# One transposing load for two pairs of expert tiles instead of one

## The reference, cut to what matters

```python
def layer0(x, t_emb, router_W, router_bias, w1, w3, w2, W1e, W2e):
    xf = x.reshape(-1, 256)                                   # 8192 tokens
    shared = silu(xf @ w1) * (xf @ w3) @ w2                   # every token
    s = sigmoid(concat([xf, tf], -1) @ router_W)              # 8 experts
    _, topk_idx = top_k(s + router_bias, 2)                   # two experts a token
    combine = ...                                             # gates of the two, which sum to 1
    y = einsum('enh,ehc->enc', gelu(einsum('nc,ech->enh', xf, W1e)), W2e)
    routed = einsum('ne,enc->nc', combine, y)
    return (shared + routed) / 3

def layer1(h, z, W, b, alpha):                                # z is the layer before's output
    def step(h, z_t):                                         # 256 steps, one after the other
        gate = sigmoid(h @ Wh.T + z_t @ Wz.T + b)
        h = tanh(h * (1 - alpha) + gate * z_t)
        return h, h

x = x + layer0(x, cond, ...)
x = x + layer1(cond, x, ...)
```

## Time and profile before

| | |
|---|---|
| time, median of 3 runs | 770.74 us (768.95 to 771.95) |
| the profiled execution | 774.02 us, of which the span of instructions is 772.1 us |
| mean granted clock of TensorE | 0.967 |
| PE busy | 711.0 us (92%) |
| DVE, ACT, POOL busy | 549.0, 472.3 and 270.6 us |
| DMA moved | 124.83 MB, 162 GB/s over the span |
| transposing loads of `xe` | 88 |

### The profile page before, as it was taken

One profiled execution on the slowest core, in us unless ns is written; L12 is line 12 of the kernel. 1 busy time (PEld: TensorE's weight loads), 2 busy tenths in 40 slices (PEclk: granted clock), 3 DMA queues, 4 the chain that ended last, 5 costly groups with the idle time before them and its releaser, 6 DMA issues.

```text
span 772.1 us, 23818 instructions
## 1 busy us (share of the span) xinstructions
PE 711.0 (92%) x8562; PEld 512.1 (66%) x8562; DVE 549.0 (71%) x2014; ACT 472.3 (61%) x1347; POOL 270.6 (35%) x284
## 2 busy tenths in 40 slices
PE   5899898998999999999989999999999999999763
PEld 3454486645788756898568896565888555686442
DVE  4787651458777698876678886897975678866754
ACT  4746464634567755677666677556876645676433
POOL 2037455166542156452075025772040173003100
PEclk9999999999999999999999999999999999999865
DMA  8836799774996675895859454357484354123101
GB/s 279 323 110 226 222 235 281 199 193 117 205 233 167 172 174 141 203 213 164 205 144 253 99 146 165 118 166 132 101 203 135 111 164 118 43 90 121 39 14 42
DMA packets 166466, 124.83 MB, mean 162 GB/s; under 512 B 118706, under 2 KB 147156, under 8 KB 166356
## 3 DMA queue, kind: packets, MB, share of 16 engines
q1 hardware_dynamic: 150436, 79.19, 42.1%
q0 software_dynamic: 14368, 41.96, 17.7%
q10 hardware_dynamic: 1552, 2.15, 0.8%
HBM read 39.90 MB, written 55.84 MB: 124 GB/s over the span
## 4 chain that ended last, share of the span: by engine, by line
PE 68%; DVE 12%; ACT 7%; DMA 6%; issue 4%; SPq 1%; POOL 1%; ACTq 0%; DVEq 0%; POOLq 0%
PE bank L1731 64%; PE bank L1930 2%; DMA xe<-x_slots_even 2%; PE bank L1865 1%; DVE full L1492 1%; DVE pre L1553 1%; DVE hid_low L1499 1%; DVE taken L1550 1%; SPq L956 1%; DMA xe<-x_slots_odd 1%; ACT th L1249 1%; ACT hs_high L1257 1%; DMA x_res<-in_x_dram 1%; POOL y_got L1129 1%; DVE r_sum L1518 1%
## 5 line engine op out<-in xcount | busy, mean ns | idle before, releaser
L1731 PE MATMUL bank<-xe,w1e_high 128*128 128x128 f16 x1360 | 216.6, 220 | 8.1 <-DMA xe<-x_slots_even 3.6
L1731 PE MATMUL bank<-xs,w_high 128*128 128x512 f16 x512 | 168.9, 385 | 5.0 <-DVE w_low L1669 2.8
L1731 PE MATMUL bank<-xe,w1e_low 128*128 128x128 f16 x680 | 146.9, 219 | 0.0
L1499 DVE TENSOR_TENSOR hid_low<-full,hid_high 128x512 f16<-128x512 f32 (+1 forms) x152 | 103.2, 679 | 45.1 <-ACT hid_high L1202 34.9
L1731 PEld LDWEIGHTS bank<-xe,w1e_high 128*128 x1360 | 114.3, 97 | 26.5 <-issue 14.0
L1249 ACT ACTIVATE th<-bank 128x64 f32<-128x64 f32 x256 | 56.9, 222 | 101.4 <-PE bank L1731 97.3
L1550 DVE SCALAR_TENSOR_TENSOR taken<-th,zq 128x64 f32<-128x64 f32 x256 | 58.2, 227 | 78.0 <-ACT th L1249 73.6
L1257 ACT ACTIVATE hs_high<-pre 128x64 f16<-128x64 f32 x256 | 65.5, 256 | 73.7 <-DVE pre L1553 62.5
L1731 PEld LDWEIGHTS bank<-hs_high,gwt_high 128*128 128x128 f16 x1024 | 70.1, 97 | 51.9 <-ACT hs_high L1257 37.5
L1070 POOL TENSOR_TENSOR fence_pool<-zero 128x1 f32<-128x1 f32 x12 | 2.8, 234 | 278.2 <-DMA y_slots_odd<-y_pair 84.7
L1731 PE MATMUL bank<-hs_high,gwt_high 128*128 128x32 f16 x1024 | 79.0, 178 | 22.5 <-ACT hs_high L1257 21.9
(11 more groups left out here) (156 smaller groups left out, 1705.8 us busy)
## 6 DMA issues: line engine op xcount, KB each, us to landing
y_slots_even<-y_pair SPq DMA_DIRECT2D x45, 256.0 KB
y_slots_odd<-y_pair SPq DMA_DIRECT2D x37, 256.0 KB
x_res<-in_x_dram SPq DMA_DIRECT2D x16, 512.0 KB
out_dram<-o_tok SPq DMA_DIRECT2D x32, 256.0 KB, 3.1
x_tok<-in_x_dram SPq DMA_DIRECT2D x14, 512.0 KB, 5.0
x_slots_even<-zeros POOLq DMA_DIRECT2D x1, 4096.0 KB, 18.1
x_slots_odd<-zeros POOLq DMA_DIRECT2D x1, 4096.0 KB, 15.2
y_got<-in_L_cond_W1e_dram SPq DMA_DIRECT2D x4, 512.0 KB, 12.9
```

What stands on the lines that cost most here:

```text
L1499: dve.tensor_tensor(hid[1][:, u.i % NR, some], full32[:, u.i % 2, some], hid[0][:, u.i % NR, some], ALU.subtract).then_inc(s_lo, 1)
L1731: return pe.matmul(out_ap, w, mov, start=start, stop=stop, skip_group_check=True)
```

## The change

One load now brings two pairs, 512 rows (the last one of a section 384, as the last pair has one tile). The ring of four pairs becomes two halves of two pairs, with one semaphore a half. Loads are issued at odd pairs only, once the second pair of the half has been read, so that the loads of pairs k + 3 and k + 4 are issued together in the unit with the odd pair k. `first_pairs` issues two loads in place of four. PE waits for the half's load ahead of each of its pairs.

```diff
-        xe = sb("xe", [P, NIN, 2, KC, 2 * P], F16)
+        xe = sb("xe", [P, NIN // 2, 2, KC, 4 * P], F16)
...
-        s_xin = [sem(f"s_xin{i}") for i in range(NIN)]
+        s_xin = [sem(f"s_xin{i}") for i in range(NIN // 2)]
...
-            def load_pair(n, p):
+            def load_pairs(n, p):
                 nth = PAIR0[n] + p
                 if nth >= NIN:
-                    sp.wait_ge(s_up, PAIR_UNIT[nth - NIN] + 1)
-                rows = P if p == PAIRS[n] - 1 else 2 * P
-                sp.dma_start_transpose(xe[:, nth % NIN].rearrange("p h k s -> p (h k) s")[:, :, 0:rows],
-                                       x_slots[n % 2][2 * p * P:2 * p * P + rows, :]).then_inc(s_xin[nth % NIN], 16)
+                    sp.wait_ge(s_up, PAIR_UNIT[nth - NIN + 1] + 1)
+                rows = 3 * P if p == PAIRS[n] - 2 else 4 * P
+                sp.dma_start_transpose(xe[:, nth // 2 % 2].rearrange("p h k s -> p (h k) s")[:, :, 0:rows],
+                                       x_slots[n % 2][2 * p * P:2 * p * P + rows, :]).then_inc(s_xin[nth // 2 % 2], 16)
             def first_pairs(n):
                 scattered(sp, n)
-                for p in range(NIN):
-                    load_pair(n, p)
+                for p in range(0, NIN, 2):
+                    load_pairs(n, p)
...
-                if u.kind == EXPERT and u.k + NIN < PAIRS[u.n]:
-                    load_pair(u.n, u.k + NIN)
-                elif u.kind == EXPERT and u.n + 1 < NS and follows(u.n + 1):
-                    if u.k + NIN == PAIRS[u.n]:
-                        scattered(sp, u.n + 1)
-                    load_pair(u.n + 1, u.k + NIN - PAIRS[u.n])
+                if u.kind == EXPERT and u.k % 2 == 1:
+                    if u.k - 1 + NIN < PAIRS[u.n]:
+                        load_pairs(u.n, u.k - 1 + NIN)
+                    elif u.n + 1 < NS and follows(u.n + 1):
+                        if u.k - 1 + NIN == PAIRS[u.n]:
+                            scattered(sp, u.n + 1)
+                        load_pairs(u.n + 1, u.k - 1 + NIN - PAIRS[u.n])
...
-                    pe.wait_ge(s_xin[up.nth % NIN], (up.nth // NIN + 1) * 16)
+                    pe.wait_ge(s_xin[up.nth // 2 % 2], (up.nth // NIN + 1) * 16)
```

More of the change, by code:

```diff
@@ L1762, in up_part @@
                 return mm(up_bank(u)[:, (h * tiles_of(u) + i) * P:(h * tiles_of(u) + i + 1) * P], w1e_s[a][k][h][:, experts[u.k % 4, i], :],
-                          xe[:, u.nth % NIN, c, k, i * P:(i + 1) * P], k == 0 and n == 0, k == 1 and n == 2)
+                          xe[:, u.nth // 2 % 2, c, k, (u.nth % 2 * 2 + i) * P:(u.nth % 2 * 2 + i + 1) * P],
+                          k == 0 and n == 0, k == 1 and n == 2)
             def down_part(u, i, h, n):
```

## The result

The changed kernel takes 789.88 us (median of 4 runs, 787.96 to 791.45) against 770.92 us before (4 runs): a ratio of 1.025, 95% interval 1.021 to 1.029. The time lies in the stated range, 3.9 us above the 786 that were forecast. The profiled execution took 790.9 us with a span of 789.0 us, 16.9 us more than the span before. The ratios further down leave out three slow executions: one of doubles_from_1_load_first (1691.87 us) and two of the kernel before (776.28 and 777.17 us).

A forecast was written before the change was run, and what follows sets the result against it. PE, busy 92% of the span, was taken to bound the kernel. Waits of 16.2 us plus 1.6 for the clock less 2.5 gave 15.3 us, on the median 770.7 a forecast of 786 us; range 775 to 800.

The forecast's parts named there:

- The shorter lead: Sections 0 to 3: even pairs' loads leave a unit later, in places behind load_res; PE waits 16.2 us more.
- The larger load: Each xe load: 512 rows take 1.3 us longer to land than 256, 5.0 us for a lone load.
- The gain: Fewer issues on SP: first_pairs of sections 3 and 4 win 1.5 and 1.0 us, together 2.5.
- The clock: TensorE: seven more waits bring one more stretch at the lower clock, +1.6 us, between 0 and 6.
- The sum: Whole kernel: 16.2 us of waits plus 1.6 for the clock, less 2.5, makes 15.3 us slower.
- Hidden or absorbed: Rival: loads land nearly as soon, later PE waits shrink; 776 us at half the waits; half absorbed (775 to 778) 0.13.
- SP's relief: Rival: fewer issues on SP remove all 4.3 us of xe waits, first_pairs gives 2.5: 764 us; faster had 0.04.
- Coalescing in the DMA engines: Rival: a load's second half costs 0.8 us instead of 1.3, some 3 us less: 783 us; chance 0.12.
- A whole second trip: Rival: 512 rows go as two loads in series, 3.67 us instead of 1.3: 793 to 803 us; chance 0.15.

The follow-up runs named there:

- doubles_from_1_load_first: Kernel before, with 512-row loads in sections 1 to 5, single loads in section 0, and load_res issued behind the loads: 769.26 us, ratio 0.9974.
- late_singles: Kernel before, its 256-row loads kept but issued two at a time at odd pairs: 783.48 us, ratio 1.0145.

## Why the prediction was right, step by step

**The shorter lead** was the main term, and it was: 16.2 us of added waits were forecast, 17.0 came. By place (forecast, then the whole wait in the trace after): pair 4 of section 1 4.0 and 4.90; of section 2 4.1 and 3.54; pair 6 of section 3 3.0 and 3.92; pair 4 of section 3 1.1 more than the 0.71 of before, and 1.49 in all. Seven places wait, where 8 to 12 were named. In section 0 the sum was right and its parts were not: PE reaches pair 14 at 141.79, where it was at 137.87, 3.9 us late for 4.0 forecast; but pair 6 waited 3.79 instead of 1.4, since its load took 10.02 us and not 7.7 (SP was held 5.36 us in that issue), and pair 8 did not wait at all.

**The larger load** was put at 1.3 us. The first one of the kernel takes 4.63 us (88.18) for 3.67: 1.0 us. late_singles gives 1.0 us a place in the mean of sections 1 to 3. The Trainium skill's fit for the GpSimd path (DMA: Bandwidth & Descriptors, section Anatomy of one DMA) had an estimated 0.6; the measurement lies between the two, and decides.

**The gain** is the step that failed. 44 fewer issues were to spare SP some 57 us, and `first_pairs` 2.5 us on the path. An issue of 512 rows takes 2.38 and 3.02 us in the median, for 1.32 and 1.50 before. The two issues of `first_pairs` take 6.47 us in front of section 3 and 6.50 in front of section 4, for 6.69 and 5.97 before. First from the kernel before (the loads' issues in ns, and `first_pairs` of section 3), then from the changed one:

```profile
L956 SPq DMA_TRANSPOSE xe<-x_slots_even x48: 1222/1322/3218, 88.3 to 586.1; - x48
L956 SPq DMA_TRANSPOSE xe<-x_slots_odd x40: 1199/1504/4567, 154.6 to 683.4; - x40
...
371.95 6.69 SPq L956 DMA_TRANSPOSE xe<-x_slots_odd  x4
```
```profile
386.64 6.47 SPq L956 DMA_TRANSPOSE xe<-x_slots_odd  x2
...
537.67 6.50 SPq L956 DMA_TRANSPOSE xe<-x_slots_even  x2
```

Added up over the trace, the 44 issues take SP 133.5 us and the 88 of before took 148.8: 15 us are spared and not 57, and in `first_pairs` next to nothing. PE's other waits did shrink by 4.1 us, but not through this: from pair 14 of section 3 to pair 0 of section 4 the changed kernel takes 76.2 us for 77.7 before, and late_singles, which has four small loads in `first_pairs`, takes 76.1 (470.30 to 546.44); from pair 15 of section 2 to pair 0 of section 3 the changed kernel takes 28.6 us for 28.7 before. That other waits gave back 4.1 us where 2.5 had been put down is luck.

**The clock** was under-sized: 1.6 us forecast, 4.0 us more of PE busy time came. Stretches of the changed kernel at 0.50, the 1.2 GHz level (length, then PE's busy time; PEclk is the third number from the end):

```profile
209.60:216.20 6.60, 4.63 (x43) 4.01 (x44) 1.63 (x7) 1.39 (x5) 0.97 (x1) 0.50 1.20 284
325.70:332.30 6.60, 5.93 (x53) 5.10 (x54) 2.02 (x7) 1.66 (x5) 0.97 (x1) 0.50 0.68 183
114.00:117.20 3.20, 2.78 (x21) 2.41 (x22) 0.00 (x0) 0.00 (x0) 0.00 (x0) 0.50 1.15 343
189.20:192.30 3.10, 3.10 (x28) 3.10 (x27) 0.69 (x1) 2.09 (x4) 0.00 (x0) 0.50 0.11 37
438.30:441.50 3.20, 3.20 (x35) 2.73 (x34) 2.20 (x7) 1.74 (x5) 0.00 (x0) 0.50 0.71 188
```

All but the one at 189.20 begin within or just behind one of the four longest waits for `xe` (ended at 211.57, 326.37, 114.42 and 436.99), and two of them are twice as long as that in the earlier trace rows. From the start of pair 6 of section 0, of pair 4 of sections 1 and 2 and of pair 6 of section 3 to that of the next pair, PE is busy 0.9, 1.5, 2.0 and 1.1 us longer than before; at 189.20, where PE had not waited for `xe` but had been busy only 1.31 us of 185.5 to 189.0, 1.2 us longer; and where before had stretches of its own, at 209.4 and at 424.4, 1.5 and 1.3 us shorter. That makes 3.9 of the 4.0 us. That the waits bring the four stretches on is read from where they lie; no experiment set it apart. In the profiles of the eight experiments, with the same matmuls, PE is busy between 708.2 and 713.2 us, so part of the 4.0 may be chance.

**The sum.** 16.9 us between the profiled spans for 15.3 forecast, 19.0 between the medians. The two differ because the execution of before that was profiled lay 3.1 us above its median, that of after 1.0.

**The rivals.** Hidden or absorbed: other waits gave back 4.1 of 17.0 us, which the lower clock took again. SP's relief: 15 us of it came, and PE's waits for `xe` grew all the same. Coalescing in the DMA engines: 1.0 instead of 1.3, at seven places some 2 us. A whole second trip: not in the load at 88.18 (4.63 us); but the load at 104.23 took 10.02 us, with SP held 5.36 us in its issue and a DMA share of 1.02 and 1.20 in 104 to 108 and 108 to 112.

## What to carry to other kernels

Count the lead of a load in units of work, from its buffer's release to its use: here, with the ring in halves of two pairs, the even pair's load left a unit later, and the transfer that had to fit into the rest was twice as large. Then read the issuing queue: a load that now stands behind a wait on that queue (here `load_res`) gets that wait's time on top, and putting it back ahead gave back some 15 of 19 us. When the lead is lengthened, leave the first burst as it is: with three issues in it `load_res` left 11.79 us after the burst's start in front of section 4, for 6.02 before.

## What had not been expected of the hardware

A transposing load of twice the rows took SP about twice the issue time where loads follow each other: 6.47 us for two of 512 rows, 6.69 for four of 256; over the whole run putting loads together saved 15 of 149 us of queue time. And of the four waits of 3.5 to 4.9 us on TensorE two were followed by 6.6 us at the lower clock and two by 3.2, while the longest wait for `xe` of before, 2.31 us, was followed by none.
